# Recurrent states written straight into the output projection's tile, and an output bias split in pieces over seven steps

## The reference, cut to what matters

```python
def step(h, xt):
    cat = jnp.concatenate([xt, h], axis=-1)
    ff1 = jnp.tanh(cat @ ff1_w.T + ff1_b)
    ff2 = jnp.tanh(cat @ ff2_w.T + ff2_b)
    t_i = jax.nn.sigmoid((cat @ ta_w.T + ta_b) * TIME_DELTA + (cat @ tb_w.T + tb_b))
    h_new = ff1 * (1.0 - t_i) + t_i * ff2
    return (h_new, h_new)
h_last, cfc_seq = jax.lax.scan(step, h0, jnp.swapaxes(ssm_out, 0, 1))
layer_out = x + cfc_out @ out_w.T + out_b
```

## Time and profile before

| | us |
|---|---|
| Median of 3 runs (1527.82 to 1564.36) | 1528.44 |
| The profiled execution's own time | 1529.22 |
| Its span on core 1, the slowest | 1527.7 |
| Spans of the other cores | 1516.3 to 1524.8 |
| The recurrence on core 1, first matmul to first projection | 761.1 to 931.2 |

### The profile page before, as it was taken

The page is one execution under the profiler, slowest core; times in us unless marked ns, Lnnn a source line. Parts: engine busy times, 40 slices in busy tenths (PEclk is TensorE's granted clock), DMA queues, the critical chain, the costliest instruction groups (busy, mean ns, idle before and its releaser), DMA issues. The chain is left out here.

```text
span 1527.7 us, 32192 instructions; the slowest of 8 cores (1516.3 to 1527.7 us)
## 1 busy us (share of the span) xinstructions
PE 1248.1 (82%) x10500; PEld 842.5 (55%) x10500; DVE 1083.5 (71%) x2122; ACT 910.8 (60%) x1336; POOL 676.3 (44%) x658
## 2 busy tenths in 40 slices
PE   1155647999999999999468885767899999998998
PEld 0033423666666666664257773545566666665644
DVE  4688988788878888783545556687787787877740
ACT  2477776778787786772223331566676767765641
POOL 1211242478677685567600444026463454633531
PEclk9995767999999999999689997899999999999999
DMA  8846353222221301224120001011011211110011
GB/s 271 297 157 229 110 206 111 36 70 70 56 55 60 82 29 42 57 56 138 40 73 3 3 3 70 28 43 65 20 70 71 84 65 47 57 56 29 29 56 55
DMA packets 40683, 118.37 MB, mean 77 GB/s; under 512 B 4388, under 2 KB 12740, under 8 KB 40520
## 3 DMA queue, kind: packets, MB, share of 16 engines
q1 hardware_dynamic: 29144, 107.10, 20.4%
q0 software_dynamic: 11376, 9.22, 3.8%
HBM read 97.17 MB, written 25.70 MB: 80 GB/s over the span
## 5 line engine op out<-in xcount | busy, mean ns | idle before, releaser
L806 PE MATMUL bank<-xqT,w1q 128*128 128x258 bf16 (+1 forms) x4352 | 586.8, 282 | 89.2 <-DVE y L1154 72.2
L806 PEld LDWEIGHTS bank<-xqT,w1q 128*128 128x128 fp8e4 x4352 | 427.1, 102 | 252.5 <-issue 114.3
L835 PE MATMUL bank<-w2q,q 128*128 128x512 fp8e4 x2112 | 533.6, 382 | 0.0
L1381 POOL TENSOR_TENSOR y<-y,Rb 128x1024 f32<-128x1024 f32 (+1 forms) x136 | 339.0, 2517 | 209.0 <-ACT Rb L1026 209.0
L1212 DVE SCALAR_TENSOR_TENSOR y<-bank,convws,y 128x256 f32<-128x256 f32 (+1 forms) x544 | 256.2, 471 | 193.0 <-ACT y L986 191.6
L986 ACT ACTIVATE y<-bank,convbs,convws 128x256 f32<-128x256 f32 (+1 forms) x544 | 296.8, 555 | 159.7 <-PE bank L806 155.8
L835 PEld LDWEIGHTS bank<-w2q,q 128*128 128x128 f16 x2112 | 205.3, 98 | 166.2 <-issue 8.5
L1154 DVE SCALAR_TENSOR_TENSOR y<-bank,convws,y 128x256 f32<-128x256 f32 (+1 forms) x544 | 253.6, 466 | 0.0
L923 ACT ACTIVATE y<-y 128x1024 f32<-128x1024 f32 (+1 forms) x136 | 140.1, 1030 | 109.2 <-DVE y L1154 107.7
L1095 DVE TENSOR_TENSOR M<-M,ab 128x1024 f32<-128x1024 f32 (+1 forms) x119 | 195.2, 1640 | 1.9 <-ACT ab L935 1.9
L945 ACT ACTIVATE q<-y,qoff 128x1024 f16<-128x1024 f32 (+1 forms) x136 | 151.4, 1115 | 24.6 <-POOL y L1381 13.2
(11 more groups left out here) (197 smaller groups left out, 1361.1 us busy)
## 6 DMA issues: line engine op xcount, KB each, us to landing
w2r<-w2T SPq DMA_DIRECT2D x28, 1024.0 KB, 6.2
w1r<-w1T SPq DMA_DIRECT2D x7, 2048.0 KB, 24.5
x1t<-xall SPq DMA_DIRECT2D x19, 512.0 KB, 3.7
basebuf<-x1t SPq DMA_DIRECT2D x17, 512.0 KB, 2.7
xg<-xall SPq DMA_DIRECT2D x16, 512.0 KB, 4.3
x1t<-x2buf SPq DMA_DIRECT2D x16, 512.0 KB, 3.4
out<-x1t SPq DMA_DIRECT2D x16, 512.0 KB, 2.6
xg<-basebuf SPq DMA_DIRECT2D x14, 512.0 KB, 4.3
```

The lines of the kernel that those rows point to most:

```text
L806: mm = pe.matmul(a_bank(n)[:, 0:tw + 2], w1q[:, c, k * P:(k + 1) * P], xqT[j % 3][:, c, 0:tw + 2], start=c == 0, stop=c == DC - 1)
L835: pe.matmul(pB[e % 2][:], q[:, qs, kh, :], w2q[:, kh, 512 * h:512 * h + 512], start=kh == 0, stop=False)
L1381: pool.tensor_tensor(v, v, Rb[:, 0:w].unsqueeze(1).to_broadcast([P, 4, w]), ALU.mult).then_inc(scaled_done, 1)
```

## The change

1. State in place. A new function state(s) gives hcur[s % 2] for s < 17 and, from step 17 on, the strided view of hC in which the state has its final place. VectorE writes into it, and TensorE's next step reads its moving operand from it. GpSimd's 24 copies, the semaphore hc_done and VectorE's waits on it are gone; the projection waits for h_done of the last step.
2. Bias split in pieces. It no longer stands in step 1. One piece each stands behind the second half of steps 8 to 14: two memsets of 512 columns, the cast of the high part's row, a cast of the other row, two subtractions of 512 columns, the last cast. The projection waits for six signals instead of four.

```diff
@@ project_out
-                pe.wait_ge(hc_done, CL)
+                pe.wait_ge(h_done, 2 * NSTEP)
                 pe.wait_ge(ow_in, 16)
-                pe.wait_ge(ob_split, 4)
+                pe.wait_ge(ob_split, 6)
@@ cfc_pool
-        hv = hC[:].rearrange('p b (c k) -> p b c k', k=CL)
-        for s in range(CW, NSTEP):
-            pool.wait_ge(h_done, 2 * s + 2)
-            pool.tensor_copy(hv[:, :, :, s - CW], hcur[s % 2][:]).then_inc(hc_done, 1)
+    def state(s):
+        if s < CW:
+            return hcur[s % 2][:]
+        return hC[:].rearrange('p b (c k) -> p b c k', k=CL)[:, :, :, s - CW]
@@ cfc_pe
-            h_in = hcur[(s + 1) % 2]
+            h_in = state(s - 1) if s else None
@@ cfc_dve
-            if s == 1:
-                bias_dve()
             for half in range(2):
-                hh = hcur[s % 2][:, 2 * half:2 * half + 2, :]
+                hh = state(s)[:, 2 * half:2 * half + 2, :]
...
-                if s >= CW + 2:
-                    dve.wait_ge(hc_done, s - CW - 1)
...
+            if s >= 8:
+                bias_dve(s - 8)
-    def bias_dve():
-        dve.memset(obhl[:], 0.0).then_inc(ob_split, 1)
-        dve.wait_ge(ob_split, 1)
-        dve.wait_ge(ob_in, 32)
-        dve.tensor_copy(obhl[0:1, :], ob32[0:1, :])
-        dve.tensor_copy(obhl[32:33, :], ob32[32:33, :]).then_inc(ob_split, 1)
-        dve.wait_ge(ob_split, 2)
-        dve.tensor_tensor(ob32[32:33, :], ob32[32:33, :], obhl[32:33, :], ALU.subtract).then_inc(ob_split, 1)
-        dve.wait_ge(ob_split, 3)
-        dve.tensor_copy(obhl[32:33, :], ob32[32:33, :]).then_inc(ob_split, 1)
+    def bias_dve(n):
+        hi, lo = ob32[0:1, :], ob32[32:33, :]
+        if n < 2:
+            dve.memset(obhl[:, 512 * n:512 * n + 512], 0.0).then_inc(ob_split, 1)
+        elif n == 2:
+            dve.wait_ge(ob_split, 2)
+            dve.wait_ge(ob_in, 32)
+            dve.tensor_copy(obhl[0:1, :], hi)
+        elif n == 3:
+            dve.tensor_copy(obhl[32:33, :], lo).then_inc(ob_split, 1)
+        elif n < 6:
+            v = slice(512 * (n - 4), 512 * (n - 4) + 512)
+            dve.wait_ge(ob_split, 3)
+            dve.tensor_tensor(ob32[32:33, v], ob32[32:33, v], obhl[32:33, v], ALU.subtract).then_inc(ob_split, 1)
+        elif n == 6:
+            dve.wait_ge(ob_split, 5)
+            dve.tensor_copy(obhl[32:33, :], lo).then_inc(ob_split, 1)
```

More of the change, by code:

```diff
@@ L351, in build_nc @@
     h_done = sem('h_done')
-    hc_done = sem('hc_done')
     ow_in = sem('ow_in')
```

## The result

The changed kernel takes 1633.9 us (median of 4 runs, 1632.24 to 1634.71) against 1527.8 for the kernel before (three runs, 1527.80 to 1528.44): a ratio of 1.069, with an interval of 1.067 to 1.071. It is 6.9% slower, outside the range of the prediction on the slow side; the forecast was 1534. The profiled execution took 1634.7 us, its slowest core, number 5, 1633.2.

A forecast was written before the change was run, and what follows sets the result against it. The recurrence was taken as a loop where each engine waits for the one before. Sum: 1529.2 - 12.45 - 3.1 - 2.1 + 0.9 + 22.1 = 1534.6, less 0.8, rounded to 1534 us; range 1509 to 1572, the forecast's own 1522 to 1548.

The forecast's parts named there:

- The bias split: Recurrence: removing it from step 1 gains 12.45 us; its pieces in steps 8 to 14 hide in VectorE's idle time.
- the upper of the two estimates: Halved bias memset and subtraction on VectorE: 0.5 and 0.7 us with a fixed part, instead of 0.46 and 0.61.
- The wait for the copy: VectorE from step 19 on: dropping 44 waits of 0.07 us each on the loop gains 3.1 us.
- The end: After the last step: the projection starts 0.14 us behind the state, without waiting for the last copy; gain 2.1 us.
- VectorE's write: State write with 48 bytes between neighbours: 0.04 us more per write, 24 times on the loop, 0.9 us.
- The third rival: VectorE's strided write is as dear as GpSimd's, TensorE's read free: 1538 us; chance 0.05.
- upper bound of 0.54: VectorE's strided write at GpSimd's 5.1 ns per element: 0.88 us, 0.54 more, 26 us over 24 steps.
- TensorE's read: Steps 18 to 40, strided moving operand: 75 ns per matmul, 0.96 us more per step, 22.1 us in all.
- As a ratio: Reading chosen for TensorE's matmul: VectorE's strided cast is 1.97 times dearer, so 38 ns becomes 75.
- As an absolute rate: Other reading for TensorE's matmul: 1.24 ns per element, 86 columns in 106 ns (113 at 1.31); chance 0.20.
- the second rival: Steps 18 to 40: TensorE full at 106 ns per matmul, 6.01 us a step, 1565.5 us; chance 0.20.
- the dearest case: The absolute rate taken at 113 ns per matmul in steps 18 to 40: 1573 us.

The follow-up runs named there:

- bias_only: The kernel before with only the bias split moved to seven steps, GpSimd's copies kept: 1514.0 us, ratio 0.990.
- state_only: The kernel before with only the direct state write, bias split still in step 1: 1646.7 us (one run).
- write_only: The changed kernel plus a GpSimd memset of hC; VectorE writes strided, TensorE always reads step 16's contiguous state: 1535.5 us (one run).
- wait_moved: The kernel before with the bias split over seven steps, copies kept, VectorE's wait for the copy once per step at its head: 1511.0 us, ratio 0.989.
- read_only: The changed kernel plus a GpSimd memset of hC; VectorE writes contiguously, TensorE always reads step 17's strided state: 1631.9 us (one run).
- the sweep: From step 18 TensorE reads a zeroed hC, column distance varied per step from 2 to 48 bytes; VectorE writes contiguously: 1561.8 us (one run).
- best: As wait_moved, but VectorE writes the last state alone straight into the projection's tile: 1512.4 us, ratio 0.990 against the kernel before.

## Why the prediction was wrong, point by point

**The bias split: right.** Foretold 12.45; `bias_only` measured 14.4 in the time and 12.3 in the recurrence, as the difference of the medians over the cores; `state_only` and the changed kernel differ by 12.4 there. On core 5 of the changed kernel it is 9.5: 8.9 gained up to the state of step 17, and 0.6 for that step's first strided write against it (4.58 us from step 17 to step 18, where the kernel before has 3.97). What is missing is the break of step 3, 2.4 net, and VectorE's two gaps, 0.6. The sum had neither. I take the stall that stood before step 2 as what covered the break in the kernel before; that was not tried by itself. The kernels with a memset ahead of GpSimd's loads have the stall no more, and yet show a break in step 3 or 4 on at most two cores each. In the changed kernel the DMA engines of core 5 are busy without a pause from 762 to 771 us, and the break ends at 771.25; in `write_only` their share drops to 0.45 from 765 to 768, and its core 5 has no break. So it may as well be a transfer to TensorE's queue that comes late behind GpSimd's loads. Neither is shown. The pieces themselves hide, as foretold; the halved memset and subtraction took 0.48 and 0.68 us, near the upper of the two estimates.

**The wait for the copy: right.** 3.1 us foretold; `wait_moved` shows the late step at 3.62 instead of 3.77, which is 3.3 over 22 steps. That the copy was never late, only the waiting itself on the loop, is what makes this fix possible.

**The end: about right.** 2.1 us foretold for the projection; 1.9 measured (0.36 instead of 2.25 behind the state).

**VectorE's write: mis-sized.** The sum had 0.04 us per write; it is 0.61. I had the right row in hand: GpSimd's copy, 5.1 ns per element with the very same step, and I set it aside because it is another engine's. VectorE's extra is 4.3 ns per line, if lines are what counts there. The third rival (0.88 us per write, 1538) describes `write_only` (0.95 us, 1535.5) well. In the changed kernel it is hidden. The 0.61 lies even a little above the upper bound of 0.54 that was taken from GpSimd's copy.

**TensorE's read: this is the step that failed.** "The nearest rows are VectorE's casts ... As a ratio it makes a matmul of 38 ns one of 75. As an absolute rate ... 106 ns (113 at 1.31), the upper bound." It is 151. Neither reading of the cast bore on TensorE, and what I called the upper bound was no bound: it was another engine's rate, for another access. GpSimd's copy, 5.1 ns per element, would have set the upper end near 440 ns, and I wrote for VectorE that it is an end and didn't use it for TensorE. `read_only` shows that this one term, with the clock that fell under it, is the whole loss.

**What hung on it.** The form of the step was right: with c = 151 ns TensorE is full, as in the second rival, and the step is 48c + 24 x 0.038 = 8.2 us. It is 9.0, because of a second term that the sum put at nothing without a reason: TensorE's clock. Reading strided, it is busy all the time and is yet granted 1.2 GHz, so the 24 state-free matmuls take 70 instead of 38 ns, 0.77 us a step. Over 23 steps: 23 x (8.2 - 3.63) = 105 from the reads, 23 x 0.77 = 18 from the clock, 0.6 for step 17's first write. With the gains of 12.3, 3.3 and 1.9 that gives 1529.2 + 123.6 - 17.5 = 1635.3, beside 1634.7 measured. This is a sum made afterwards, with the measured 151 and 70 ns put in. The chance of being over 2% slower had been put at 0.21, and the dearest case at 1573.

**A slip in the sums.** The prediction says that the kernel is slower than before from about 64 ns per matmul on. By its own terms that is 68: gains of 17.65 less 0.9 for the write, over 23 steps, allow 0.73 us more a step, 4.36 = 32c + 2.19. It changed no range.

**The rule on lines.** The Trainium skill, "Advanced Engine Details and Errata", section "SBUF Cachelines", was right in kind: 16-byte lines, a penalty for a new line at each access. I used it only as a sign. Its "at least two hits on a cacheline" for full speed doesn't hold for TensorE in bfloat16: with two columns per line (8 bytes apart) a matmul takes 79 ns, with four (4 bytes apart) about 40. For VectorE's write of 172 elements four per line cost 0.36 us against 0.34, two cost 0.54.

## What to carry to other kernels

Count the 16-byte lines, not only the elements, when TensorE reads a tile with a step; VectorE's strided write was dearer still. A bfloat16 moving operand with 8 bytes between columns doubled the matmul here, with 16 or more it was four times as long, and the engine that saved work (a copy on an idle GpSimd, 42 us that nobody waited for but the first projection, 2 us) was not the one that paid. A copy on an idle engine that turns a contiguous tile into a strided one can be the cheapest thing in the loop; what is worth removing is the wait for it on the loop. And where no row shows an access on an engine, another engine's rate is no upper bound: here the range would have had to reach as far as the dearest row with that access, GpSimd's, or a small kernel would have had to measure the access first.

## What the runs showed of the hardware that was not expected

- The moving operand of a matmul costs 1.8 ns per 16-byte line touched, down to the boundary: the same pairs of columns take 78 ns inside a line and 154 across its edge. At 16 bytes between columns the cost is the same at both clock levels (154 ns at 0.97, 155 at 0.50).
- VectorE's strided write of 172 elements takes 0.95 us instead of 0.34 at 48 bytes. Between 4 and 16 bytes it grows by 0.093 us for every 2 bytes, which is 4.3 ns per line if lines are what counts; that was tried for TensorE only.
- TensorE, without any idle time but slowed by strided reads, is granted the 1.2 GHz level (0.50 from 836 to 1035 us), and the sweep shows the clock come back in contiguous steps behind such reads: 0.59 over the first contiguous batch and 1.00 after it (941.7 on), 0.54 over nearly a whole step elsewhere (871 to 875).
- Aligned pairs 96 bytes apart take 105 ns where 16, 32 and 48 bytes take 79. Not explained.
- A break in TensorE's queue after 16 matmuls of step 3 (1.71 us on core 5 of the changed kernel, 1.04 to 2.80 on the profiled cores of `wait_moved` and `bias_only`), with nothing in the profile that it waits for. It is there on six, six, five and four of the eight cores of the changed kernel, `bias_only`, `wait_moved` and `best`, and on no core of the two kernels with the longer stall before it. Not explained.
